# Attention scores in units of one PSUM bank: 22 units per batch element in place of 32

## The reference

```python
scores = jnp.einsum('bqhrd,bkhd->bhrqk', q, k) * scale
scores = jnp.where(causal, scores, jnp.finfo(scores.dtype).min)
probs = jax.nn.softmax(scores, axis=-1)
y = jnp.einsum('bhrqk,bkhd->bqhrd', probs, v)
```

## Time and profile before

| | us |
|---|---|
| three timed runs | 1441.99, 1444.25, 1444.91 |
| median | 1444.25 |
| the profiled execution | 1446.64 |
| its span, first to last instruction | 1445.1 |
| one attention stage, first score to first `early` product (fifth of eight) | 52.8 |
| 32 units' exponentials in it, first to last start | 45.1 |

### The profile page before, as it was taken

One profiled execution on the slowest core, in us unless ns is written; L12 is line 12 of the kernel. 1 busy time (PEld: TensorE's weight loads), 2 busy tenths in 40 slices (PEclk: granted clock), 3 DMA queues, 4 the chain that ended last, 5 costly groups with the idle time before them and its releaser, 6 DMA issues. The chain is left out here.

```text
span 1445.1 us, 23043 instructions
## 1 busy us (share of the span) xinstructions
PE 1213.7 (84%) x6560; PEld 763.6 (53%) x6560; DVE 1072.1 (74%) x2491; ACT 866.7 (60%) x1608; POOL 462.5 (32%) x276
## 2 busy tenths in 40 slices
PE   5974689878898889978898888988899889888697
PEld 4641155545554556545556465645556456555465
DVE  2656977699767897589876997679875998579711
ACT  2625355586547866488555866488664876378342
POOL 0003910096003830068100950048200770039300
PEclk8986589999999999999999999999999999999899
DMA  6102100020002100020001200021000300011000
GB/s 234 67 16 74 44 8 8 24 102 1 16 16 75 44 16 2 16 90 30 16 10 44 82 1 16 16 75 44 16 2 16 102 15 9 1 63 56 7 1 8
DMA packets 18545, 53.68 MB, mean 37 GB/s; under 512 B 4960, under 2 KB 5848, under 8 KB 18016
## 3 DMA queue, kind: packets, MB, share of 16 engines
q1 hardware_dynamic: 16112, 43.40, 9.3%
q0 software_dynamic: 1280, 4.20, 1.0%
q10 hardware_dynamic: 1008, 4.38, 0.8%
HBM read 45.40 MB, written 2.38 MB: 33 GB/s over the span
## 5 line engine op out<-in xcount | busy, mean ns | idle before, releaser
L1396 DVE TENSOR_TENSOR_SCAN probs_T<-bank,probs_T 128x512 f32<-128x512 f32 x256 | 304.9, 1212 | 40.8 <-ACT bank L997 28.5
L435 POOL TENSOR_TENSOR probs_T<-step_space,probs_T 128x1024 f32<-128x1024 f32 x120 | 281.8, 2357 | 0.0
L556 PEld LDWEIGHTS bank<-w_w,hidden 128*128 128x128 f32 x2048 | 243.4, 192 | 65.7 <-issue 62.0
L544 PE MATMUL bank<-hT,w_w 128*128 128x512 f32 x512 | 256.2, 620 | 16.8 <-ACT hidden L852 16.8
L556 PE MATMUL bank<-w_w,hidden 128*128 128x128 f32 x2048 | 247.4, 276 | 9.7 <-DVE step_space L1378 6.2
L852 ACT ACTIVATE hidden<-bank,w_b 128x512 f32<-128x512 f32 x256 | 171.1, 686 | 133.5 <-PE bank L544 132.3
L433 POOL TENSOR_TENSOR probs_T<-step_space,probs_T 128x512 f32<-128x512 f32 x16 | 22.4, 1417 | 700.2 <-DVE step_space L1386 700.2
L925 ACT ACTIVATE probs<-bank,row_neg 128x128 f32<-128x128 f32 (+3 forms) x256 | 135.0, 528 | 166.8 <-DVE row_neg L1247 147.6
L997 ACT ACTIVATE bank<-step_space,a_neg 128x512 f32<-128x512 f32 x256 | 168.4, 683 | 71.0 <-DVE probs_T L1396 62.0
L1247 DVE TENSOR_REDUCE row_neg<-bank 128x1 f32<-128x128 f32 (+3 forms) x256 | 122.6, 485 | 91.4 <-PE bank L640 86.1
L638 PE MATMUL bank<-k_pad,q_lat 128*128 128x512 f32 (+3 forms) x512 | 185.5, 449 | 5.4 <-DMA k_pad<-xc 5.4
(11 more groups left out here) (174 smaller groups left out, 1591.8 us busy)
## 6 DMA issues: line engine op xcount, KB each, us to landing
probs_T<-b_rows_dram SPq DMA_DIRECT2D x64, 512.0 KB, 3.7
w_w<-in_w_dram ACTq DMA_DIRECT2D x2, 2048.0 KB, 13.3
k_pad<-xc SPq DMA_DIRECT2D x64, 64.0 KB, 2.0
x_in<-in_x_dram POOLq DMA_DIRECT2D x8, 256.0 KB, 3.3
gate<-gate_rows_dram SPq DMA_DIRECT2D x1, 2048.0 KB, 7.3
out_dram<-x_out POOLq DMA_DIRECT2D x8, 256.0 KB, 2.9
step_space<-in_wmod_dram SPq DMA_DIRECT2D x1, 768.0 KB, 5.8
probs_T<-in_wqT_dram SPq DMA_DIRECT2D x1, 512.0 KB, 4.0
```

What stands on the lines that cost most here:

```text
L435: ins = nc.gpsimd.tensor_tensor(inject[:, n % 3, :, :], u[:], row.unsqueeze(1).to_broadcast([P, DH, T]), ALU.mult)
L544: mm(hid1_bank(n)[:], w["w1"][:, n // C1, n % C1 * P:(n % C1 + 1) * P], hT[3][:], start=True, stop=True).then_inc(hid1_mm.sem, 1)
L556: ins = mm(bank[OUT1_BANK[e]][:, t * P:(t + 1) * P], hidden[:, (e * C1 + c) % (2 * C1), t * P:(t + 1) * P], w["w2"][:, e * C1 + c, :], sta ...
L1396: v.tensor_tensor_scan(state[:, n % 2, c, :], decay(DH * n + c)[:], inject[:, n % 3, c, :], 0.0, ALU.mult, ALU.add).then_inc(st_ok.sem, 1)
```

## The change

A unit now fills a bank. In query tile 0 the four heads of a group make one unit (4 blocks), in tile 1 two heads make one (2 x 2 blocks); tiles 2 and 3 keep a head to a unit (3 and 4 blocks). That is 11 units a group, 22 in all. A wide unit has one score product with 512 columns, one mask product with the mask repeated, one row maximum over two or four rows of columns, as many exponentials as it has heads, four transposes and one copy. LAG, the ring of four and the two banks stay. All the numbers at which side work hangs are set anew, and which engine copies which unit is now a list (eight units by VectorE, fourteen by ScalarE).

```diff
-        row_neg = sb("row_neg", [P, 4])
+        row_neg = sb("row_neg", [P, 4, HG])
...
-        UNITS = G * NT * HG
+        unit_of = [(g, i, j, width) for g in range(G) for i, width in enumerate((4, 2, 1, 1)) for j in range(0, HG, width)]
+        UNITS = len(unit_of)
...
-        BY_ACT = [n for n in range(UNITS) if n % 2 or n < ALL_BY_ACT]
-        BY_DVE = [n for n in range(UNITS) if n not in BY_ACT]
+        BY_ACT = [n for n in range(UNITS) if n not in BY_DVE]
...
         def transposed(n):
-            i, j = n // HG % NT, n % HG
-            return (probs_T[:, j, 0:i + 1, i * P:(i + 1) * P],
-                    bank[4 + n % 2][:, 0:(i + 1) * P].rearrange("p (k q) -> p k q", q=P))
+            g, i, j, width = unit_of[n]
+            if width == 1:
+                return (probs_T[:, j, 0:i + 1, i * P:(i + 1) * P],
+                        bank[4 + n % 2][:, 0:(i + 1) * P].rearrange("p (k q) -> p k q", q=P))
+            if i == 0:
+                return (probs_T[:, :, 0, 0:P], bank[4 + n % 2][:].rearrange("p (j q) -> p j q", q=P))
+            return (probs_T[:, j:j + width, 0:i + 1, i * P:(i + 1) * P],
+                    bank[4 + n % 2][:].rearrange("p (j k q) -> p j k q", j=width, q=P))
...
                 def scores(n):
-                    g, i, j = n // (NT * HG), n // HG % NT, n % HG
+                    g, i, j, width = unit_of[n]
...
-                    mm(s[:, 0:(i + 1) * P], q_lat[:, g, i * P:(i + 1) * P], k_pad[:, g, j, 0:(i + 1) * P],
-                       start=True, stop=False)
-                    mm(s[:, i * P:(i + 1) * P], ident_bf[:], mask_bf[:], start=False, stop=True).then_inc(s_mm.sem, 1)
+                    if width == 1:
...
+                    else:
+                        to = s[:].rearrange("p (j k) -> p j k", j=width)
+                        mm(to, q_lat[:, g, i * P:(i + 1) * P], k_pad[:, g, j:j + width, 0:(i + 1) * P],
+                           start=True, stop=False)
+                        mm(to[:, :, i * P:(i + 1) * P], ident_bf[:], mask_bf[:].unsqueeze(1).to_broadcast([P, width, P]),
+                           start=False, stop=True).then_inc(s_mm.sem, 1)
...
-                    for k in range(i + 1):
+                    for k in range(width * (i + 1)):
                         ins = tr(bank[4 + n % 2][:, k * P:(k + 1) * P], probs_ring[:, n % 4, k * P:(k + 1) * P], ident[:])
...
-                    for n in range(8 * half + 4, 8 * half + 8):
+                    for n in range(HALF_END[half] - 3, HALF_END[half]):
                         taken(pe, b, n)
...
-                    if n in (12, 20, 28):
-                        values(n // 8 - 1)
+                    if n in PE_VALUES:
+                        values(PE_VALUES.index(n))
...
-                    if n >= UNITS // 2 and n % 8 == 1:
-
-                        act.wait_ge(y_mm.sem, y_mm.at(b, n // 8 - 1))
+                    if n >= UNITS // 2:
+                        act.wait_ge(y_mm.sem, y_mm.at(b, 1 if n < HALF_END[2] else 2))
...
-                    f(probs_ring[:, n % 4, 0:(i + 1) * P], bank[SCORE_BANK[n % 4]][:, 0:(i + 1) * P], ACT.Exp,
-                      bias=row_neg[:, n % 4:n % 4 + 1], accum_out=row_sum[:, g, i, j:j + 1]).then_inc(s_exp.sem, 1)
+                    for k in range(width):
+                        at = slice(k * (i + 1) * P, (k + 1) * (i + 1) * P)
+                        ins = f(probs_ring[:, n % 4, at], bank[SCORE_BANK[n % 4]][:, at], ACT.Exp,
+                                bias=row_neg[:, n % 4, k:k + 1], accum_out=row_sum[:, g, i, j + k:j + k + 1])
+                    ins.then_inc(s_exp.sem, 1)
...
-                    v.reduce_max(row_neg[:, n % 4:n % 4 + 1], bank[SCORE_BANK[n % 4]][:, 0:(i + 1) * P], AX_X,
-                                 negate=True).then_inc(s_max.sem, 1)
+                    source = bank[SCORE_BANK[n % 4]][:, 0:width * (i + 1) * P].rearrange("p (j k) -> p j k", j=width)
+                    v.reduce_max(row_neg[:, n % 4, 0:width], source, AX_X, negate=True).then_inc(s_max.sem, 1)
...
-NORM_UNITS = 7
-PRE_UNIT = 21
-ALL_BY_ACT = 12
+NORM_AT = {7: (0, 4), 8: (4, 8), 9: (8, 11), 10: (11, 14)}
+PRE_AT = {n: (2 * (n - 18), 2 * (n - 17)) for n in range(18, 25)}
 LAG = 3
-LAST_SUM, LAST_READ, PE_MIXER, DVE_MIXER, FINISH, TAKE_X, NORM_UNIT = 3, 2, 6, (3, 7), 5, 8, 8
-
-PE_HEAD, ACT_HEAD, DVE_HEAD = (16, 18, 25, 28), (17, 22, 26), (20, 23, 32)
+
+HALF_END = (3, 11, 14, 22)
+BY_DVE = (7, 9, 11, 12, 14, 16, 18, 20)
+PE_VALUES, ACT_INVERSE, DVE_WIDEN, DVE_NORMALISE = (7, 14, 18), (8, 15, 19), (4, 12, 17, 23), (10, 16, 21)
+LAST_SUM, LAST_READ, PE_MIXER, DVE_MIXER, FINISH, TAKE_X = 3, 1, 5, (2, 6), 4, 7
+PE_HEAD, ACT_HEAD, DVE_HEAD = (11, 13, 16, 18), (12, 15, 17), (14, 16, 22)
...
-SETUP_PE, SETUP_DVE, SETUP_ACT = (4, 9, 14), (6, 11, 18), 16
+SETUP_PE, SETUP_DVE, SETUP_ACT = (2, 5, 9), (3, 6, 12), 11
```

More of the change, by code:

```diff
@@ L637, in scores @@
                     s = bank[SCORE_BANK[n % 4]]
-                    mm(s[:, 0:(i + 1) * P], q_lat[:, g, i * P:(i + 1) * P], k_pad[:, g, j, 0:(i + 1) * P],
-                       start=True, stop=False)
-                    mm(s[:, i * P:(i + 1) * P], ident_bf[:], mask_bf[:], start=False, stop=True).then_inc(s_mm.sem, 1)
+                    if width == 1:
+                        mm(s[:, 0:(i + 1) * P], q_lat[:, g, i * P:(i + 1) * P], k_pad[:, g, j, 0:(i + 1) * P],
+                           start=True, stop=False)
+                        mm(s[:, i * P:(i + 1) * P], ident_bf[:], mask_bf[:], start=False, stop=True
+                           ).then_inc(s_mm.sem, 1)
+                    else:
+                        to = s[:].rearrange("p (j k) -> p j k", j=width)
+                        mm(to, q_lat[:, g, i * P:(i + 1) * P], k_pad[:, g, j:j + width, 0:(i + 1) * P],
+                           start=True, stop=False)
+                        mm(to[:, :, i * P:(i + 1) * P], ident_bf[:], mask_bf[:].unsqueeze(1).to_broadcast([P, width, P]),
+                           start=False, stop=True).then_inc(s_mm.sem, 1)
                 def transposes(n):
-                    i = n // HG % NT
+                    g, i, j, width = unit_of[n]
                     pe.wait_ge(s_exp.sem, s_exp.at(b, n + 1))
@@ L932, in iteration @@
                         f(a_exp[:], w["a_log"][:], ACT.Exp).then_inc(setup_a, 1)
-                    if n in (13, 21, 29):
-                        take_inverse(n // 8 - 1)
+                    if n in ACT_INVERSE:
+                        take_inverse(ACT_INVERSE.index(n))
                 for n in range(UNITS - LAG, UNITS):
@@ L1246, in row_maximum @@
                         dve.wait_ge(s_exp.sem, s_exp.at(b, n - 3))
-                    v.reduce_max(row_neg[:, n % 4:n % 4 + 1], bank[SCORE_BANK[n % 4]][:, 0:(i + 1) * P], AX_X,
-                                 negate=True).then_inc(s_max.sem, 1)
+                    source = bank[SCORE_BANK[n % 4]][:, 0:width * (i + 1) * P].rearrange("p (j k) -> p j k", j=width)
+                    v.reduce_max(row_neg[:, n % 4, 0:width], source, AX_X, negate=True).then_inc(s_max.sem, 1)
                 def take_transposed(n):
                     dve.wait_ge(p_T.sem, p_T.at(b, n + 1))
-                    if n >= UNITS // 2 and n % 8 == 0:
-                        dve.wait_ge(y_mm.sem, y_mm.at(b, n // 8 - 1))
+                    if n >= UNITS // 2:
+                        dve.wait_ge(y_mm.sem, y_mm.at(b, 1 if n < HALF_END[2] else 2))
                     to, source = transposed(n)
@@ L1278, in attend @@
                         row_maximum(n)
-                    if n in (9, 17, 25, 33):
-                        widen(n // 8 - 1)
-                    if n in (15, 23, 31):
-                        normalise(n // 8 - 1)
+                    if n in DVE_WIDEN:
+                        widen(DVE_WIDEN.index(n))
+                    if n in DVE_NORMALISE:
+                        normalise(DVE_NORMALISE.index(n))
                     if n - LAG in BY_DVE:
                         take_transposed(n - LAG)
-                    if n == 6 and not behind:
+                    if n == 3 and not behind:
                         take_x(b)
-                    if ahead and PRE_UNIT <= n:
-                        if n - PRE_UNIT < NORM_STEPS:
-                            norm_step(b + 1, 0, n - PRE_UNIT, x_in, chain_pre)
+                    if ahead:
+                        for k in range(*PRE_AT.get(n, (0,))):
+                            norm_step(b + 1, 0, k, x_in, chain_pre)
                     if behind:
@@ L1296, in attend @@
                             take_x(b)
-                        if NORM_UNIT <= n < NORM_UNIT + NORM_UNITS:
-                            for k in range(2 * (n - NORM_UNIT), min(2 * (n - NORM_UNIT + 1), NORM_STEPS)):
-                                norm_step(b - 1, 3, k, x_mid, chain_norm)
+                        for k in range(*NORM_AT.get(n, (0,))):
+                            norm_step(b - 1, 3, k, x_mid, chain_norm)
                         if n in DVE_HEAD:
```

2 lines of the change are left out of this document (1 added, 1 removed).

## The result

The changed kernel takes 1451.91 us (median of 5 runs, 1450.64 to 1456.47) where the kernel before, run beside it, takes 1444.25 (5 runs, 1441.54 to 1447.32). The ratio is 1.0055 [1.0036, 1.0074]: slower by 0.55%, where I had forecast no difference. The range (1435 to 1452) just holds the time. The profiled run took 1450.64 us about a span of 1448.9, against 1446.64 about 1445.1 before, so the two traces account for 3.8 us.

The account below looks back on a forecast made before the run. Each attention stage was held bound by a ladder of hand-offs through VectorE, with TensorE fullest (45.0 of 52.8 us). 6 x 0.1 - 0.4 = + 0.2 us on 1444.25, leaned towards gain, gave 1443.8; range 1435 to 1452.

Parts of the forecast that it names:

- the change doesn't do what it says: Rival: four-row maxima or repeated mask cost 0.2 us more each, cancelling the 0.64 us saving; no chance of its own.
- Step 1: Stage start: the scan's last read comes 0.7 us later, but TensorE waits about 0.2 us for it instead of 1.39.
- Step 2: VectorE up to the expert layer's `xn`: on time at 713.0; TensorE waits 1.6 us before `values`, 2.2 before `xn`.
- Step 3: Router on TensorE: exponentials before the modulation and a held score delay it to 717.3, + 0.9 us.
- Step 4: Choice: unit 14's score, its maximum and a copy now precede it, so it starts at 720.1, + 1.2 us.
- Step 5: Tanh and gates: one exponential before the tanh where two stood; gates' transposes at 726.2 or 726.4, + 0.3 us.
- Step 6: b2's product, needing `gates_T`: starts at 729.6 again behind a 0.5 us wait; last score ends near 735.2 as before.
- Step 7: Stage end: four norm steps instead of two before the last inverse's transpose, + 0.4 us against up to 0.4 won earlier.
- The first stage: First attention stage, starting at 1.2 GHz: four narrow units take 2.57 us, a wide one 2.14, so - 0.4 us once.
- The last stage: Eighth attention stage: no change, because no next batch follows it.
- The clock: Rival: TensorE's new waits make its clock fall once a stage, 7 x 1.65 = + 11.6 us, 1456; chance 0.06.
- Coarse hand-offs: Rival: VectorE's 1.5 us of waits before `xn` don't vanish, 7 x 1.1 = + 7.7 us, 1452; chance 0.18.

Follow-up runs that it names:

- e8: The kernel before, narrow units, plus five unused 512-column products while TensorE waits for the first keys; 1439.57 us, ratio 0.9972.
- e3: The changed kernel with steps of the next batch's norm moved forward, two instead of four before the copy ahead of the last inverse; 1451.79 us, ratio 1.0047.
- e1: The changed kernel plus unused TensorE products filling the waits before the transposes of `xn` and of the gates; 1440.7 us, ratio 0.9962.
- e10: The kernel before, narrow units, with gates' transposes, modulation, tanh, choice, gates and the copy of b2's product moved sooner; 1440.7 us, ratio 0.998.
- e9: e7 with VectorE's copy of `expert_sum` at unit 18 instead of 22 and more of the next batch's norm early; 1410.34 us, ratio 0.9775.
- e6: e2 with the first `values` one unit later, and ScalarE modulating ahead of two 256-column exponentials; 1422.14 us, ratio 0.9852.
- e7: e6 with choice, tanh, gates and the gates' transposes each one unit sooner; 1418.28 us, ratio 0.9816.
- e2: The changed kernel with the transposes of `xn` and of the gates one unit later on TensorE; 1437.4 us, ratio 0.9946.
- e11: e9 plus five unused 512-column products while TensorE waits for the first keys; 1410.52 us, ratio 0.9759.

## Why the prediction was wrong, point by point

The third stage of the changed kernel, at full clock, is where the walk can be held against the trace. Its first score starts at 347.64, where the walk began at 690.33, so 342.69 is to be added. TensorE's timeline:

```profile
350.79 1.13 PE L606 MATMUL bank<-probs,w_ident 128*128 128x512 f32 x2
...
361.82 0.86 PE L683 MATMUL bank<-probs_T,v_lat 128*32 128x256 f32 x16 [1.68 <-DVE x_mid L1149]
...
370.58 0.66 PE L533 MATMUL bank<-w_ident,xn 128*128 128x128 f32 x4 [2.16 <-DVE xn L1212]
...
374.90 1.06 PE L541 MATMUL bank<-w_wg,hT 128*128 128x8 f32 x8 [0.86 <-ACT hT L871]
...
383.90 0.60 PE L595 MATMUL bank<-w_ident,gates 128*8 128x128 f32 x4 [2.38 <-DVE gates L1183]
...
387.23 1.15 PE L600 MATMUL bank<-w_b,gates_T 8*128 8x128 f32 x8 [0.43 <-ACT gates_T L898]
...
396.51 0.44 PE L667 MATMUL bank<-w_ident,hidden 128*128 128x128 f32 x2 [0.61 <-DVE hidden L1276]
```

and VectorE's, same columns:

```profile
349.52 1.21 DVE L1096 TENSOR_TENSOR probs<-probs_T,bank 128x1024 f32<-128x1024 f32 x1
...
376.91 0.56 DVE L1263 TENSOR_REDUCE row_neg<-bank 128x1 f32<-128x384 f32 x1 [2.24 <-PE bank L646]
377.38 0.68 DVE L1270 COPY probs_T<-bank 128x512 f32<-128x512 f32 x1
377.98 0.18 DVE L1156 COPY logits<-bank 128x32 f32<-128x32 f32 x1
```

- **The units.** VectorE's groups by shape in that stage (count, busy us, mean ns of one, idle before):

```profile
L1263 DVE TENSOR_REDUCE row_neg<-bank 128x1 f32<-128x512 f32 x8 | 5.5, 691 | 2.5 <-PE bank L646 2.0 <-DVE x_mid L1149 0.2
...
L1263 DVE TENSOR_REDUCE row_neg<-bank 128x4 f32<-128x512 f32 x2 | 1.4, 690 | 1.3 <-PE bank L652 1.3
```

  A maximum over four heads costs what one head of 512 columns does, as taken. The rival that the change doesn't do what it says is out. VectorE's busy time is 41.5 against 41.6 us before, less of a saving than the 0.5 that I had worked out (0.64 of maxima less 0.1 of copies). The score I had costed at nothing; e8's first narrow scores start 0.33 to 0.38 apart at full clock, four of them some 1.35 us, and a wide one with its mask 1.08 (347.64 to 348.72). That is a saving for TensorE, which stood waiting anyway. By the figure of the Trainium skill (Perfetto Trace Analysis, Optimizing Scalar/DVE Operations: about 125 ns of fixed cost for an operation on PSUM) VectorE would have saved an estimated 1.25 us a stage; no row shows that.
- **The waits before.** I wrote that all of TensorE's waits in the earlier trace rows end at VectorE. That reading was wrong: 1.8 of the 6.7 us that they list end at ScalarE's copies.
- **Step 1, the start:** right. The last read starts at 349.52, that is 692.21 (forecast 692.25), and no wait stands at TensorE's use of it, where 1.39 us stood.
- **Step 2, `xn`:** right. Waits of 1.68 and 2.16 (forecast 1.6 and 2.2), transposes at 713.27 (713.2).
- **Step 3, the router:** 717.59, forecast 717.3. Right but for 0.3.
- **Step 4, the choice:** 720.67, forecast 720.1; + 1.7 where I had + 1.2. VectorE stands 2.24 us before the maximum ahead of it: the score of that unit is queued behind the late router on TensorE. This term was mis-sized, and steps 5 and 6 inherit it.
- **Step 5, the gates:** 726.59, forecast 726.2 to 726.4, with a wait of 2.38 us.
- **Step 6, b2's product:** 729.92, forecast 729.6 behind a wait of 0.5; measured 0.43.
- **Step 7, the end:** the inverse at 739.20 against 738.59. The last score's second pass had been 0.2 late by then, so the end added 0.4, as forecast, but steps 2 to 6 had lost 0.2 where I let them win up to 0.4. The stage is + 0.6 and not + 0.1. The reason that I gave for the end, four steps ahead of one transpose, doesn't hold as such: e3 took them away and the time stayed.
- **The first stage:** forecast - 0.4, measured - 5.5. I had priced the shorter TensorE sequence at the low clock and not asked whether the low clock would last as long. e8 shows that 4.3 of it go with the clock, and e1 and e10 that the clock's share changes from one execution to the next.
- **The last stage:** put at nothing because it has no next batch; it is 1.2 longer at full clock (e1: 50.88 against 49.65), since steps 2 to 6 are in it as in the others.
- **The clock,** a rival at 0.06: this is the step that failed. The sum has no term for it, and the falls cost 6.9 us. I had its condition in hand, since the walk itself gave the waits of 2.2 and 2.8 us, and its price: 11.6 us at one fall a stage. It came in five stages, not seven, at 1.1 to 1.25 us for a stage with one fall and 1.7 for one with two, not 1.65 for each. That a fall costs less than the 1.65 may be because part of it lies under work that waits for VectorE; no run tests this. The case was rated low because one row of a 4.5 us wait was all that bore on it; waits half as long were new in this kernel, and with no row for them the chance should have been near even.
- **Coarse hand-offs,** a rival at 0.18 with 1452: its time was hit but its mechanism only in part. Its condition, that more than 0.7 us of VectorE's waits stay in step 2, isn't met: after the last read VectorE's maxima wait for no score until `xn`, which was on time. The delay arose at the choice. The rule of the Trainium skill that stands beside it (Perfetto Trace Analysis, Optimizing Scalar/DVE Operations: where VectorE or ScalarE isn't full and makes others wait, breaking instructions up may help) fits the first order, in which wide units are slower (1.0055), but not the last: with the moves, wide units stand at 0.9775 and narrow ones at 0.998.

Taken together: + 0.6 instead of + 0.1 in each of stages 3 to 7, - 0.5 in the second, 1.2 in the last instead of nothing, + 6.9 by the clock instead of nothing, - 5.5 instead of - 0.4 in the first stage. Two errors of about 7 and 5 us had opposite signs, so the forecast was nearer than its reasoning.

## What to carry to other kernels

When units of work are made wider, the order of the side work that hangs on their numbers must be set anew: here the same wide units are 0.5% slower with the order that came with them and 2.3% faster with another. Walk each engine's queue to find the waits that a change makes new, and treat a new wait of TensorE of 2 us as a possible fall of its clock as well as a delay. Where work stands in a stretch in which its engine has no gap, moving it inside that stretch brings nothing; moving it out of the stretch brought most of its length (0.8 of 1.1 us in e9).

## What the runs showed of the hardware

- The granted clock fell to 1.2 GHz for 3.4 us, at times 6.8, in stages with TensorE waits of 1.7 to 2.7 us that are otherwise busy. A fall of 3.4 us cost 1.1 to 1.6 us (the most in e10's seventh stage), two in a stage 1.7, one of 6.8 us 2.3. In e6, e7 and e9, whose longest wait in the middle stage is 1.2 us or less, no stage from the third on has one.
- The same waits don't always bring it. The changed kernel's third stage has 2.4, 2.2 and 1.7 us and keeps the full clock; its fourth has one fall, its fifth two. e2 has the router's wait of 1.6 or 1.7 in each stage from the second on and falls in four of them; e1's 1.7 us before the first `values` is never followed by one; and e10's one fall comes in a stage whose waits, 1.4 us at most, the stages beside it have too. What decides between them these runs don't settle, nor which of two waits brings a given fall.
- At the start of the first stage, behind a wait of 4.8 to 5.9 us for the first keys, the clock was low for 6.8 to 13.7 us under narrow units and 3.4 to 10.2 us under wide ones. Both ends of the second range have the same instructions there (the changed kernel and e1), and so have both ends of the first (e10 and the kernel before). Of the two kernels with five products in that wait, e8 (narrow) had 3.4 us of it and e11 (wide) none.
- Work that nobody reads can pay: e1 gives TensorE 3.6 us more in a stage and the kernel is 11 us faster by the medians, 7.5 by the profiled spans, than without it; 6.9 us are the falls that are gone.
